# A causal attention layer on one core: masking the diagonal score tiles that share a PSUM bank with one VectorE addition and one plain maximum

## What is computed

```python
q = (x @ Wq).reshape(B, C, H, D).transpose(0, 2, 1, 3)      # k and v alike, x is layer-normed
scores = jnp.einsum('bhqd,bhkd->bhqk', q, k)
scores = jnp.where(causal, scores, -jnp.inf)
attn = jax.nn.softmax(scores / jnp.sqrt(jnp.float32(E)), axis=-1)
ctx = jnp.einsum('bhqk,bhkd->bhqd', attn, v)
...
x = x + ctx @ Wo + bo
x = x + quantised(layernorm(x)) @ quantised(weight).T + bias
```

## Time and profile before

| | us |
|---|---|
| median of 3 runs | 2093.06 (2091.07 to 2094.66) |
| the profiled execution | 2085.36 |
| its span | 2083.6 |
| PE busy | 1980.0 (95%) |
| DVE busy | 1716.6 (82%) |
| ACT busy | 1351.9 (65%) |
| POOL busy | 810.7 (39%) |

### The profile page before, as it was taken

How to read it: one execution, slowest core, us unless ns; L and a number is a source line. 1 busy time by engine, 2 the same in 40 slices (tenths; PEclk the granted TensorE clock), 3 DMA queues, 4 the chain that set the end, 5 groups by cost and what they waited for, 6 DMA issues and landing times.

```text
span 2083.6 us, 35416 instructions
## 1 busy us (share of the span) xinstructions
PE 1980.0 (95%) x11749; PEld 755.4 (36%) x11749; DVE 1716.6 (82%) x4358; ACT 1351.9 (65%) x2881; POOL 810.7 (39%) x1123
## 2 busy tenths in 40 slices
PE   6799899999999999999999999999999999999984
PEld 3333333333333343434334343433333433333433
DVE  4797886869887978796897879797889899888875
ACT  5357566767766767676766666666766666677661
POOL 3323414231335554553243646453345444211232
PEclk9999999999999999999999999999999999999997
DMA  4442221414041241703323161340614121130000
GB/s 155 123 111 64 77 68 38 102 48 120 9 123 55 74 99 38 174 11 81 93 53 95 46 140 50 79 102 17 160 39 112 54 55 40 39 90 24 9 31 21
DMA packets 162963, 152.04 MB, mean 73 GB/s; under 512 B 32982, under 2 KB 150492, under 8 KB 162780
## 3 DMA queue, kind: packets, MB, share of 16 engines
q1 hardware_dynamic: 162780, 149.77, 27.0%
HBM read 91.89 MB, written 57.02 MB: 71 GB/s over the span
## 4 chain that ended last, share of the span: by engine, by line
PE 71%; DVE 19%; ACT 3%; issue 3%; POOL 2%; SPq 2%; DMA 1%; POOLq 0%; ACTq 0%; DVEq 0%
PE psum L1496 20%; PE psum L1479 19%; PE psum L1464 16%; DVE max_parts L1201 8%; PE psum L1560 8%; PE psum L1553 5%; DVE psum L1196 4%; ACT probs L1005 2%; SPq L674 1%; PE psum L1531 1%; DVE max_parts L1196 1%; ACT acc_sb L1014 1%; PE psum L1582 1%; PE psum L1523 1%; DVE stats L1259 1%
## 5 line engine op out<-in xcount | busy, mean ns | idle before, releaser
L1005 ACT ACTIVATE probs<-psum 128x512 f32<-128x512 f32 (+3 forms) x2560 | 1211.6, 536 | 518.9 <-PE psum L1479 511.8
L1201 DVE TENSOR_REDUCE max_parts<-psum 128x1 f32<-128x512 f32 x1536 | 965.2, 682 | 123.6 <-PE psum L1464 119.5
L1479 PE MATMUL psum<-q_rows,k_rows 99*128 99x512 bf16 (+3 forms) x2560 | 856.1, 351 | 3.3 <-ACT probs L1005 1.9
L1464 PE MATMUL psum<-k_rows,q_rows 96*128 96x512 bf16 (+3 forms) x2560 | 815.7, 349 | 30.2 <-DVE max_parts L1201 11.4
L1496 PE MATMUL psum<-probs,v_in 128*17 128x512 f32 (+3 forms) x5120 | 594.3, 536 | 11.9 <-ACT acc_sb L1014 11.5
L1196 DVE CUSTOM_DVE_ANT_0 psum<-psum,causal 128x128 f32<-128x128 f32 (+3 forms) x1024 | 476.5, 518 | 135.5 <-PE psum L1464 132.7
L1479 PEld LDWEIGHTS psum<-q_rows,k_rows 99*128 99x128 bf16 x2560 | 237.2, 97 | 640.5 <-ACT probs L1005 500.3
L833 POOL TENSOR_SCALAR_AFFINE_SELECT probs<-probs 128x512 f32<-128x512 f32 x256 | 165.9, 648 | 727.3 <-ACT probs L1005 727.1
L1464 PEld LDWEIGHTS psum<-k_rows,q_rows 96*128 96x128 bf16 x2560 | 244.6, 98 | 291.7 <-DVE max_parts L1201 81.8
L1496 PEld LDWEIGHTS psum<-probs,v_in 128*17 128x17 f32 x5120 | 86.1, 95 | 226.7 <-issue 162.1
L1196 DVE DVE_READ_ACCUMULATOR2_ANT max_parts<- 128x1 f32 x1024 | 144.9, 141 | 0.0
(11 more groups left out here) (161 smaller groups left out, 1268.7 us busy)
## 6 DMA issues: line engine op xcount, KB each, us to landing
q_rows<-qk_scratch SPq DMA_DIRECT2D x384, 64.0 KB, 2.7
k_rows<-qk_scratch SPq DMA_DIRECT2D x384, 64.0 KB, 2.7
qk_scratch<-shop SPq DMA_DIRECT2D x56, 384.0 KB, 3.2
sums_scratch<-acc_sb SPq DMA_DIRECT2D x48, 256.0 KB, 2.3
shop<-in_L_attn_x SPq DMA_DIRECT2D x19, 512.0 KB, 5.2
v_scratch<-shop SPq DMA_DIRECT2D x16, 544.0 KB, 4.3
v_in<-v_scratch SPq DMA_DIRECT2D x64, 136.0 KB, 2.6
out_shop<-in_L_attn_x SPq DMA_DIRECT2D x12, 512.0 KB, 8.5
```

Source lines behind the costliest of these rows:

```text
L1005: nc.scalar.activation(probs[s % NPROBS][:, h, a:CHUNK], bank[SCORE_BANKS[n % 3]][:, a:CHUNK], ACT.Exp, scale=SCALE).then_inc(probs_ready, 1)
L1201: nc.vector.tensor_reduce(max_parts[k % 2][:, first:first + heads, t % TILES, c], ring_bank(UNIT_USE[n])[:, 0:heads * width] .rearrange("p ...
L1464: ins = nc.tensor.matmul(dst[:, i * width:(i + 1) * width], q_rows[u][0:ROWS, qc, first + i, t % TILES * P:(t % TILES + 1) * P], k_rows[u] ...
L1479: nc.tensor.matmul(bank[SCORE_BANKS[n % 3]][:, a:CHUNK], k_rows[u][0:ROWS + LEVELS, h, kb * P:(kb + 1) * P], q_rows[u][0:ROWS + LEVELS, qc ...
```

## The change

Diagonal units that hold one head (j = 2 and 3) keep the `tensor_tensor_reduce`. Those that hold four or two heads (j = 0 and 1) get one `tensor_tensor` addition over the last 128 columns of every head, the triangle broadcast over the heads, written back to PSUM; VectorE waits for it through `link`; then they fall through to the plain `tensor_reduce` of the full units, over all 512 columns of the bank with one result for each head. The wait for the constants moves ahead of the branch, for unit 0 alone. In the changed kernel L1195 is the masked maximum, L1204 the addition, L1205 the plain maximum.

```diff
--- before.py
+++ after.py
@@ -1188,16 +1188,20 @@
                 k, t, c, first, heads = UNITS[n]
                 width = unit_width(n)
                 dve.wait_ge(unit_ready, n + 1)
+                if n == 0:
+                    dve.wait_ge(consts_ready, 1)
+                if c == QCS[k] and heads == 1:
+                    mine = ring_bank(UNIT_USE[n])[:, 0:width]
+                    nc.vector.tensor_tensor_reduce(
+                        out=mine, in0=mine, in1=causal[:, CHUNK - width:CHUNK], scale=1.0, scalar=LOWEST, op0=ALU.add,
+                        op1=ALU.max, accum_out=max_parts[k % 2][:, first, t % TILES, c:c + 1]).then_inc(unit_used, 1)
+                    return
                 if c == QCS[k]:
-                    if n == 0:
-                        dve.wait_ge(consts_ready, 1)
-                    for i in range(heads):
-                        mine = ring_bank(UNIT_USE[n])[:, i * width:(i + 1) * width]
-                        ins = nc.vector.tensor_tensor_reduce(
-                            out=mine, in0=mine, in1=causal[:, CHUNK - width:CHUNK], scale=1.0, scalar=LOWEST, op0=ALU.add, op1=ALU.max,
-                            accum_out=max_parts[k % 2][:, first + i, t % TILES, c:c + 1])
-                    ins.then_inc(unit_used, 1)
-                    return
+
+                    mine = ring_bank(UNIT_USE[n])[:, 0:heads * width].rearrange("p (h n) -> p h n", h=heads)
+                    mine = mine[:, :, width - P:width]
+                    triangle = causal[:, None, CHUNK - P:CHUNK].broadcast_to([P, heads, P])
+                    link(nc.vector.tensor_tensor(out=mine, in0=mine, in1=triangle, op=ALU.add))
                 nc.vector.tensor_reduce(max_parts[k % 2][:, first:first + heads, t % TILES, c],
                                         ring_bank(UNIT_USE[n])[:, 0:heads * width]
                                         .rearrange("p (h n) -> p h n", h=heads), AX.X, ALU.max).then_inc(unit_used, 1)
```

## The result

The changed kernel takes 2110.53 us, the median of 6 runs (2107.79 to 2114.4), against 2092.07 for 6 runs of the kernel before (2088.73 to 2094.66): 18.5 us more, a ratio of 1.0092 with a 95% interval of 1.0075 to 1.0108. Forecast were 2109 us and 16 us more. The profiled execution took 2108.0 us, its span is 2106.1.

A forecast was written before the change was run, and what follows sets the result against it. TensorE was taken as the bound, VectorE a close second. VectorE's 65 us extra (0.37 + 0.64 = 1.01 us a block, 64 blocks), 25% passed on, gave 16 us on the 2093.06 median: 2109 us, range 2095 to 2131.

The forecast's parts named there:

- What bounds the kernel: Whole program: TensorE, busy 1980.0 of 2083.6 us, sets the pace; VectorE, 1716.6, is a close second through ring-bank waits.
- What the change removes: VectorE's masked maxima at j = 0 and 1: 0.95 + 1.48 = 2.43 us a block, priced by steps.
- What it adds: VectorE's addition, wait and plain maximum: 1.32 us at j = 0, 1.06 a unit at j = 1.
- VectorE's busy time: Sign in the profile after: near 1716.6 + 59 us, being 65 less 0.03 of idle at each of 192 waits.
- The 65 us of steps: VectorE's net extra engine time: 1.01 us more a block over 64 blocks; bounds 42 and 76 us.
- TensorE's busy time: Sign in the profile after: about the same, with its waits for VectorE longer by some 16 us.
- What reaches the end: At TensorE's ring-bank waits: 25% of VectorE's 65 us comes through, 16 us; the rest is hidden by idle time.
- The chance of 71%: Chance given to the forecast for the whole kernel, slower by 5 to 38 us.
- Durations count, so it is faster: Rival at VectorE's changed units: listed durations hold the engine, 40 us saved, 10 passed on, 2083 us; chance 7%.
- All hidden: Rival: VectorE's idle time ahead of the changed units absorbs the addition, 0 to 4 us more, 2093 to 2097; chance 15%.
- VectorE as the bound: Rival: VectorE busy 1782 us, most of the 65 us comes through, more than 38 us, up to 2158; chance 7%.

The follow-up runs named there:

- experiment 3: Changed kernel with all 704 diagonal units, one-head units too, given addition then plain maximum: 2190.38 us against 2089.09 for the kernel before.
- Experiment 4: Kernel before, with plain maxima and no mask at j = 0 and 1 in the first pass: 2081.0 us against 2089.09.
- 6: Kernel before, with no mask in the first pass at all, plain maxima everywhere: 2077.26 us against 2089.63.
- experiment 12: Kernel before, plus one scrap VectorE maximum over 192 columns ahead of each of 256 j = 2 masked maxima: 2114.4 us against 2090.32.
- 1: Changed kernel with the 128 j = 1 units back on masked maxima, so j = 0 alone changed: 2101.76 us against 2089.09 for the kernel before.
- 2: Changed kernel with the 64 j = 0 units back on masked maxima, so j = 1 alone changed: 2102.68 us against 2089.09 for the kernel before.
- 5: Changed kernel with masked maxima kept from block 16 on, so only the first 16 of 64 blocks changed: 2100.32 us against 2089.63 for the kernel before.
- 10: Changed kernel with only blocks 16 to 63 changed, the first 16 keeping masked maxima: 2104.18 us against 2090.32 for the kernel before.

## Why the prediction was right

**What bounds the kernel.** TensorE with VectorE close behind, joined by the ring of four banks: shown by the chain and the waits after the change, and by experiments 3 and 4, which change nothing but VectorE's work and move the time both ways.

**What the change removes.** 0.95 and 1.48 us a block from the steps in the order of time, not 1.86 and 2.36 from the durations. Experiment 4 bears this out: replacing the same masked maxima by plain ones was priced at -40 us from the steps; VectorE's busy time fell by 38.2. From the durations it would have been 1.86 - 0.68 and 2.36 - 1.36 a block, -140 us.

**What it adds.** Every term held within 0.02 us: additions of 0.697 and 0.425 us against 0.69 and 0.43, the wait 0.034 against 0.03, the step of a j = 1 unit 1.06 against 1.06. The write to PSUM costs no more than one to SBUF (697 ns against the 692 of L1241), and a maximum with four or two results is listed with 693 ns, one with one result with 681. The claim of the Trainium skill, VectorE: DVE Perf Modes, The DRAIN you can't avoid, that a semaphore between Vector instructions costs nothing extra, does not hold here: behind a wait for the instruction just before it, one starts 34 ns after that one's end, without such a wait some 80 ns ahead of it, so the wait costs about 0.11 us. The prediction read the rest of that section too narrowly: the Trainium skill adds there that a next instruction that is not held starts earlier, and the overlap of 80 ns in the earlier trace rows agrees with that rather than denying it.

**VectorE's busy time** was forecast to rise by 59 us and rose by 50.4. The 65 us of steps are close to what the trace has, some 67; I took off too little for converting to busy time. In the union of spans an instruction's tail, which reaches past its step, counts only where the engine goes idle behind it. A masked group's last read reaches further than a maximum's tail, and with less idle time there are fewer tails: with each overlap counted for the later instruction alone, the changed units hold 56 us more and all the rest of VectorE's work 5.6 us less. No term of the forecast time hung on that conversion.

**TensorE's busy time** was to stay about the same. It rose by 13.2 us, of 22.5 between the spans (by 8.0 against the second profile of the kernel before, 1985.2). That sign of being right failed. An estimate of where it comes from: a matmul of 512 columns is listed with 0.38 us and the next starts 0.22 later, so each further wait lets some 0.16 us more count as busy. The weight loads' waits for VectorE went from 254 to 308, 54 x 0.16 = 9 us; the lower clock adds some 6.

**What reaches the end.** 25% of 65 us, 16 us, from the share of VectorE's lines on the chain (18 to 20%) and a guess upward. Measured: 18.5 us (16 to 23), 28%. At 20% the forecast would have been 13 us, outside that interval, and no row gave the size of the guess: that part came near by luck. The chain's share is that of a small change from here, and the two experiments that take load away stay near it: 21% and 20% of VectorE's busy time (4 and 6). Added load lies above it: 37% in the change (18.5 of 50.4), 44% in experiment 12, 60% in experiment 3 (101 of 170). So the share rises with the load, as I held it in experiment 3.

The partial changes don't fit in a line: 60%, 41%, 78% and 38% of 21.0, 33.5, 13.7 and 37.0 us (1, 2, 5, 10). The granted clock goes with the difference. Over the 124 runs for which a clock is on record, within one kernel, a run whose mean granted clock is lower by 0.001 takes 1.2 us longer (standard error 0.1). The runs of j = 0 alone and of the first batch alone had the low means named in 1 and 5, and by that slope 3.2 and 4.0 us of their loss go with the clock; 9.5 and 6.7 us are left, 45% and 49%. For j = 1 alone and blocks 16 to 63 (0.9838 and 0.9847) the same correction gives 40% and 41%, for experiment 12 39%. So the four parts come to lie between 40% and 49%, and their sums fall to 23 and 22 us. For the changed kernel (0.9822, against 0.9832 to 0.9839 for the kernel before) it takes off 1 to 2 us; a gap of some 5 us between parts and whole stays, about the size of the noise of three medians. Which is cause and which effect the runs don't tell: a low stretch lengthens a run, and a longer stall may bring one.

**A slip in the numbers.** The chance of 71% was given to 5 to 38 us more, but the range starts at 2095, which is 2 us more than 2093.06; the stretch from 2 to 5 us had no chance of its own. The measured 18.5 lies well inside either.

**The rivals.** Durations count, so it is faster: refuted by the steps and the result; with it the rule of the Trainium skill (the same page, Rules for kernel authors) to minimise the number of Vector instructions, which here took 640 away and lost 18.5 us. All hidden: refuted by the result. The idle time ahead of L1204 is still 80.6 us, yet unused; as I read it, because it comes before the unit and not behind it. VectorE as the bound: not at this size; experiment 3 shows what it looks like.

## What to carry to other kernels

Price an instruction on an in-order engine by the step from its start to the next one's in a stretch without idle time, not by its listed duration; several short fused passes may be cheaper than two long ones. Where an engine feeds another through a small ring, a delay on it costs a share of itself even though it is idle for a sixth of the time: the chain of waits gives that share for a small change (here some 20%, which taking load away bore out), added load passes on more than that (here 37 to 60% of VectorE's added busy time, the clock's part included), and releasing a bank later costs time even when the engine does less.

## What the runs showed of the hardware

The granted clock of TensorE fell to half for stretches of 3 to 10 us, in the kernel before as well, 7 us in one execution and 17 in another of the same program; the sum of matmul steps puts 2.5 and 5.7 us on them. In the changed kernel one such stretch begins within a wait of 2.47 us for VectorE. I had not counted on the clock in a kernel whose TensorE is busy for 95%, but it cost less than it seems: the second profile of the kernel before, with 10 us more at the low clock, was 2.1 us longer. The 124 runs agree: 0.001 less of mean granted clock is 4.2 us more at the low one over 2090 us, and goes with 1.2 us. In the two partial changes with the lowest clock that makes 3 to 4 us, enough to distort a share. Whoever compares versions that lie 5 us apart in 2100 reads the granted clock of every run beside its time.
